# Order of halves in the first turn and at the router's first step, another schedule for the pieces of the late shared experts, and shared parts added by one transfer

## The reference, cut to what matters

```
x = x + cross_attention(layernorm(x), ctx)          # 16 query heads, 8 key/value heads of 128, 256 context rows
h = layernorm(x)
scores = sigmoid(h @ gate_w.T); sc = scores + gate_bias      # 32 experts in 4 groups
group_scores = top2 of each group, summed; keep the 2 best groups; topk_idx = best 4 experts
topk_w = scores[topk_idx] / sum * 2.0
experts: at most 128 rows each, (silu(h @ w1[e]) * (h @ w3[e])) @ w2[e], weighted by topk_w
shared:  (silu(h @ shared_gate) * (h @ shared_up)) @ shared_down
x = x + experts + shared
```

## Time and profile before

| | us |
|---|---|
| median of three runs | 1691.13 |
| profiled execution | 1686.83 |
| its span, first to last instruction | 1685.1 |
| PE busy | 1618.0 (96%) |
| DVE busy | 1223.4 (73%) |
| POOL busy | 887.6 (53%) |
| ACT busy | 787.4 (47%) |
| mean granted clock of TensorE | 0.991 of full speed |

### The profile page before, as it was taken

The page is one execution under the profiler, slowest core; times in us unless marked ns, Lnnn a source line. Parts: engine busy times, 40 slices in busy tenths (PEclk is TensorE's granted clock), DMA queues, the critical chain, the costliest instruction groups (busy, mean ns, idle before and its releaser), DMA issues. The chain is left out here.

```text
span 1685.1 us, 34839 instructions
## 1 busy us (share of the span) xinstructions
PE 1618.0 (96%) x12194; PEld 1153.3 (68%) x12194; DVE 1223.4 (73%) x3498; ACT 787.4 (47%) x1986; POOL 887.6 (53%) x1188
## 2 busy tenths in 40 slices
PE   6999999999999999999999999999999999999983
PEld 4767677777777777767676767776776766555541
DVE  6887676767676776767676777777777765787872
ACT  5764444435343444444443544445454433565551
POOL 2444544545463636464545463646455356677773
PEclk9999999999999999999999999999999999999997
DMA  7654433344344434343335544445454385799974
GB/s 233 184 143 79 89 80 80 82 76 96 64 96 76 96 61 92 70 102 67 80 74 97 93 95 92 102 95 108 90 112 83 88 319 155 207 281 281 275 194 59
DMA packets 394461, 204.12 MB, mean 121 GB/s; under 512 B 347808, under 2 KB 356000, under 8 KB 394288
## 3 DMA queue, kind: packets, MB, share of 16 engines
q1 hardware_dynamic: 380416, 180.27, 44.4%
q0 software_dynamic: 13312, 20.57, 6.6%
q10 hardware_dynamic: 560, 1.05, 0.2%
HBM read 87.15 MB, written 31.36 MB: 70 GB/s over the span
## 5 line engine op out<-in xcount | busy, mean ns | idle before, releaser
L961 ACT ACTIVATE arena<-arena,neg_max 128x256 f32<-128x256 f32 x512 | 253.7, 496 | 384.7 <-DVE neg_max L1260 331.5
L690 POOL TENSOR_SCALAR arena<-arena,prob_scale 128x256 f16<-128x256 f32 x384 | 184.5, 496 | 461.2 <-DVE prob_scale L1269 447.1
L1260 DVE CUSTOM_DVE_ANT_0 arena<-ps_score,mask_add 128x256 f32<-128x256 f32 x512 | 186.6, 421 | 141.7 <-PE ps_score L1606 141.7
L1604 PE MATMUL ps_query<-xn_both,arena 128*128 128x256 f16 x1024 | 279.2, 273 | 1.6 <-DMA xn_both<-xn_half 1.6
L1606 PE MATMUL ps_query<-xn_both,arena 128*128 128x256 f16 x1024 | 279.1, 273 | 0.0
L1605 PE MATMUL ps_query<-xn_both,arena 128*128 128x256 f16 x1024 | 279.1, 273 | 0.0
L1275 DVE SCALAR_TENSOR_TENSOR arena<-arena,prob_scale 128x256 f16<-128x256 f32 x384 | 233.0, 654 | 8.2 <-POOL arena L690 8.2
L1604 PE MATMUL ps_out<-arena,o_t 128*128 128x512 f16 x512 | 194.1, 379 | 0.7 <-DVE o_t L1280 0.7
L1605 PE MATMUL ps_out<-arena,o_t 128*128 128x512 f16 x512 | 194.0, 379 | 0.0
L1606 PE MATMUL ps_out<-arena,o_t 128*128 128x512 f16 x512 | 194.0, 379 | 0.0
L745 POOL DMA_INDIRECT slot_table<-entry,slot_at x128 | 133.2, 1041 | 48.2 <-issue 33.4
(11 more groups left out here) (319 smaller groups left out, 4110.7 us busy)
## 6 DMA issues: line engine op xcount, KB each, us to landing
arena<-w SPq DMA_DIRECT2D x96, 512.0 KB
x_in<-x SPq DMA_DIRECT2D x16, 512.0 KB, 4.0
xn_rows<-xn_half SPq DMA_DIRECT2D x15, 512.0 KB, 3.1
out_rows_dram<-x SPq DMA_DIRECT2D x30, 256.0 KB
ctx_in<-ctx_t SPq DMA_DIRECT2D x16, 256.0 KB, 3.1
weight_in<-wq SPq DMA_DIRECT2D x8, 512.0 KB, 5.8
weight_in<-wo SPq DMA_DIRECT2D x8, 512.0 KB, 4.6
arena<-arena SPq DMA_TRANSPOSE x256
```

The lines of the kernel that those rows point to most:

```text
L690: pool.tensor_scalar(p_rows[:, c, 0, :], probs[:, c, :], prob_scale[:, c:c + 1], 1.0, ALU.mult, ALU.mult).then_inc(norm_hi, 1)
L961: act.activation(probs[:, c, :], probs[:, c, :], ACT.Exp, bias=neg_max[:, c:c + 1], scale=-1.0, accum_out=prob_sum[:, c:c + 1]).then_inc(e ...
L1260: dve.tensor_tensor_reduce(out=probs[:, c, :], in0=ps_score[h][:, t * S:(t + 1) * S], in1=mask_add[b % 2][:, :], scale=-SCORE_SCALE, scala ...
L1604: pe.matmul(dst, a.hi, b.hi, start=start and n == 0, stop=False)
```

## The change

Six things change.

1. The first turn. x of sequence 0 is loaded as two transfers, so that its first rows can be measured alone. ctx_low(0) goes behind xn_rest. PE does value(0,0,0) before scores(0). value_low and ctx_low(1) of the first turn go from before prob_scales to behind it: the first behind prob_scales, the other two behind key_low(1). ACT does the second value_high behind scale_last.
2. The order of `jobs`: of wq and wo for the same head, wq is loaded and split first.
3. In every turn head_low(i-1) is done after two of the three low halves of the probabilities (late_head is gone).
4. At j = 3 choose_0 and choose_1 are done after query_low and key_low instead of around query_low.
5. The pieces: two up pieces instead of one before the two down pieces of the sequence before. NOT_BY_POOL and the orders of DVE, ACT and POOL around it follow. POOL does record(z-1, 1) after six splits and the first expert_high instead of first. The first gather is used after piece 20 instead of after piece 21. Pieces beside experts lie in steps with e % 8 != 7, so e = 0 to 21; the shared parts n = 5, 6 are added in step 22.
6. add_shared is one transfer of 256 rows instead of two of 128.

```diff
 for _n in range(len(LATE)):
-    PIECES.append(("u", _n, 0))
+    PIECES += [("u", _n, f) for f in range(2)]
     PIECES += [("d", _n - 1, t) for t in range(TB)] if _n else []
-    PIECES += [("u", _n, f) for f in range(1, FSB)]
+    PIECES += [("u", _n, f) for f in range(2, FSB)]
...
-NOT_BY_POOL = (10, 13, 14, 15, 16)
+NOT_BY_POOL = (10, 11, 14, 15, 16)
...
-    if _e % 4 != 3 and EARLY + len(BESIDE) < len(PIECES):
+    if _e % 8 != 7 and EARLY + len(BESIDE) < len(PIECES):
...
             def add_shared(n):
-                for t in range(TB):
-                    r = LATE[n] * T + t * P
-                    pool.wait_ge(staged, TB * n + t + 1)
-                    if t == 0:
-                        pool.wait_ge(out_rows, 16 * TB * (LATE[n] + 1))
-                        if n > 2:
-                            pool.wait_ge(added, adds_before["s", n])
-                    pool.dma_start(out[r:r + P, :], shared_y[n % 2][t], accum_op=ALU.add).then_inc(
-                        added if n else added_first, 16)
+                r = LATE[n] * T
+                pool.wait_ge(staged, TB * (n + 1))
+                pool.wait_ge(out_rows, 16 * TB * (LATE[n] + 1))
+                if n > 2:
+                    pool.wait_ge(added, adds_before["s", n])
+                pool.dma_start(out[r:r + T, :].rearrange("(t p) d -> p t d", p=P), shared_both[n % 2],
+                               accum_op=ALU.add).then_inc(added if n else added_first, 16)
...
 (pool_program, after the last turn)
             z = B - 1
-            record(z - 1, 1)
             for k in range(3):
                 late_split(k)
             inv_std(1, z, x1_stats, x1_rstd, x1_normed)
-            for k in (3, 4):
+            for k in (3, 4, 5):
                 late_split(k)
-            for e in range(2):
-                expert_high(e)
-            for k in range(7, 10):
+            expert_high(0)
+            record(z - 1, 1)
+            expert_high(1)
+            for k in (8, 9):
                 late_split(k)
...
 (dve_program, a turn)
-                if i == 0:
-                    value_low(ps_fill[1], 0, 0, 0)
-                    value_low(ps_fill[0], 0, 0, 1)
-                    ctx_low(1)
...
-                if i and not late_head:
-                    head_low(i - 1)
+                if i == 0:
+                    value_low(ps_fill[1], 0, 0, 0)
                 if live:
                     probs_low(i, range(0, CELLS // 2))
-                if i and late_head:
+                if i:
                     head_low(i - 1)
                 if live:
                     probs_low(i, range(CELLS // 2, CELLS - 1))
-                if j == 3 and routed:
-                    choose_0(z)
                 if i + 1 < TURNS:
                     query_low(i + 1)
-                if j == 3 and routed:
-                    choose_1()
...
                 if i + 1 < TURNS and not early_key:
                     key_low(i + 1)
+                if i == 0:
+                    value_low(ps_fill[0], 0, 0, 1)
+                    ctx_low(1)
+                if j == 3 and routed:
+                    choose_0(z)
+                    choose_1()
...
 (pe_program, after the last turn; act_program the same with copy_rows)
-            for k in range(11, EARLY):
+            for k in range(11, EARLY - 1):
                 piece(k)
-            for e in range(2):
-                expert_rows(e)
+            expert_rows(0)
+            piece(EARLY - 1)
+            expert_rows(1)
```

More of the change, by code:

```diff
@@ L830, in pool_program @@
                 gather(e)
-            for k in range(19, EARLY):
+            for k in (20, 21):
                 late_split(k)
@@ L1438, in dve_program @@
                 xn_rest(0, t)
+            ctx_low(0)
             for n in (0, 1):
@@ L1486, in dve_program @@
                     find_slots(z)
-                late_head = i < TURNS and first(b, j) is not None and first(b, j)[0] in ("value", "down")
                 if live:
@@ L1541, in dve_program @@
             piece(4)
-            for part in (0, 1, 2):
+            piece(5)
+            for part in (0, 1):
                 expert_low(0, part)
@@ L1826, in pe_program @@
                 b, j = divmod(i, KV)
+                if i == 0:
+                    filler(("value", 0, 0, 0), ps_fill[1])
                 if i < TURNS:
```

56 lines of the change are left out of this document (33 added, 23 removed).

## The result

The changed kernel takes 1702.86 us (median of four runs, 1700.55 to 1703.7) beside 1691.43 of the kernel before: ratio 1.0067, 95% interval 1.005 to 1.0085. It is 11 us slower, where 1684 was forecast. The profiled executions are 1700.55 (span 1698.8) against 1686.83 (1685.1), 13.7 apart.

A forecast was written before the change was run, and what follows sets the result against it. The prediction took TensorE, busy for 96% of the span, plus its idle stretches to bound the kernel. Its terms, 0 + 9.5 - 4.8 - 11.9 = -7.2 us, applied to the 1691.1 median gave 1684 us, range 1671 to 1695.

The forecast's parts named there:

- First turns: Start of attention: earlier second scores not kept, since project(0) waits for head_low; 0, from -3 to +3 us.
- Late head: Attention turns, mainly from b=10: head_low behind two probability halves holds project until 2.48 us after GpSimd's start; +18.8 us.
- Choose behind the key: Attention at j=3 of b=10 to 15: the 1.00 us wait of the next scores goes; -6.0 us.
- the attend waits: Inside attention: waits for the turned probabilities, 3.4 us, shrink as the turns before them get longer; -3.3 us.
- Router's last step: Between attention and experts: splits ahead of records bring the first expert from 1425.4 to 1420.6; -4.8 us.
- Experts: Expert steps to the end: fewer losses in the first 22 steps, faster accumulating transfers behind; -11.9 us, bounds 0 and -18.
- (1): Rival, groups after e=22: adds bind the bare steps, each us of spacing above 9.5 costs 5; 1696 us, chance 0.22.
- (3): Rival, router and start: gather chain doesn't move, start loses 2 us to a fallen clock; 1691 us, chance 0.11.
- (2): Rival, attention: late head is cheap, gaining up to 9.3 us, sum -20 or more; 1668 us, chance 0.10.
- (4): Rival, attention: VectorE's low and GpSimd's high halves hinder each other, 0.2 us a turn, +5; 1689 us, chance 0.07.

The follow-up runs named there:

- late_only: Kernel before with only head_low(i-1) put behind two low halves of the probabilities in every turn; ratio 1.0109 to the kernel before, +18.6 us.
- combo_old_start: combo with the first turn, the load of x and the order of weight jobs of the kernel before; ratio 0.9943 to the kernel before.
- choose_only: Kernel before with only choose_0 and choose_1 put behind query_low and key_low at j = 3; ratio 0.9959 to the kernel before, -7 us.
- changed_again: The changed kernel run again without an edit, beside the other follow-up runs; ratio 1.0080 to the kernel before.
- second pair: Traces of the unedited changed kernel and kernel before, both run again in the follow-ups; ratios 1.0080 and 1.0005 to the kernel before.
- old_steps: Changed kernel with pieces back in the steps of the kernel before (e % 4 != 3), shared parts n = 5, 6 in step 26; ratio 1.0043.
- combo_old_steps: combo with pieces in the steps of the kernel before (e % 4 != 3), shared parts in step 26; ratio 0.9915 to the kernel before.
- bare_20: Changed kernel with step 20 also left without a piece; ratio 1.0038 to the kernel before.
- piece21_first: Changed kernel with piece 21 put back before the first rows on TensorE and ScalarE; ratio 1.0062 to the kernel before.
- combo: Changed kernel with head_low back in its early place, step 20 without a piece and piece 21 before the first rows; ratio 0.9914 to the kernel before.

## Why the prediction was wrong

- **First turns, 0.** Within its bounds (+0.9 us at scores(8) by the first pair of traces, 0.0 by the second), and by the reason given: the lead of scores(1), 2.1 us for the 3.1 forecast, isn't kept, since project(0) and its followers wait for head_low. So 0 is a gain of 2 to 3 us by the new start less as much for the late head, as late_only and combo_old_start show.
- **Late head, +18.8.** Right in place: 2.47 to 2.49 us in each bound turn. In size it is right where it is part of the changed kernel (next point). That late_only's runs give +18.6 is in part luck: the 18.8 is a sum before the 3.3 us of waits that go with it, so 15.5 was to be compared with 18.6 (interval 15.6 to 20.9), and the traces show 13.6. What the Trainium skill's page "SBUF — State Buffer", section "Who interferes with whom", would make of it, by the prediction's estimate about 2.7, isn't what the turns show; with both engines at it project came 2.47 to 2.49 behind.
- **Choose behind the key, -6.0, and the attend waits, -3.3.** Right together: choose_only -7; scores(80) to (127) +8.1 in the changed kernel and +8.3 in changed_again, for 17.9 - 9.3 = 8.6. Attention as a whole came to +11.3 for +9.5, and to +9.5 in the second pair.
- **Router's last step, -4.8: failed,** +2.5 in the first pair, -1.9 in the second. What failed is the sentence that the first gather's rows land at about 1416.8, 3.9 us behind their issue, with TensorE there 1.6 us before. From issue to rows it was 7.2 (changed) and 6.9 (changed_again). In the kernel before it was 6.1 already (1416.88 to 1423.0), and TensorE came just as the rows landed, so no wait showed it. TensorE then stood 4.96 or 3.66 us ahead of the rows, with piece 21, 2.6 us of ready work, queued right behind them, and its clock fell. From the first copy to the first tanh it was 4.4 us before, 7.5 after. By terms, from scores(127): the gather was forecast at 65.5, its rows at 69.4 and the first tanh at 75.9. The first trace has it issued 1.9 later, landing 3.3 slower and the tanh another 2.1 later, 7.3 in all; the second -1.6, +3.0 and +1.4, or 2.7. So the landing was mis-sized by 3 us in both; the late issue, behind the split of piece 17, was in the first alone. With the piece ahead of the rows the step gains 4.0 (76.5 for 80.5).
- **Experts, -11.9: failed,** 0 in the first pair, +1.6 in the second. Two terms. The first 22 steps were put at 166.0 and took 172.9: I had counted bare steps only as room for additions and not asked what stands between the last hidden row and its down piece; with no bare step there GpSimd's split is late, 5.98 us and the clock behind it. The rest from step 22 was put at 81.8 and took 86.6 (1698.8 less 1612.2): the shared additions were issued at 11.7 for 9, and landed in 16.4 for 13; the six pairs behind them and the end came as forecast. 6.9 + 4.8 is 11.7 of the 11.9. That the stage came out at 0 is itself a sum: the dense steps lost some 4 us against old_steps, and the rest of the change seems to have given as much back.
- **The rivals.** (1), the additions bind the bare steps, did not come by its own measure: the five distances behind the first pair were 9.4 us on average, (1687.33 - 1640.36)/5, where it priced what lies above 9.5. What was long was the landing of the shared ones ahead of them. And yet combo_old_steps shows that the schedule is worth nothing with the additions in the way: what the wait in step 20 costs less, the end takes back in part. (3) is what the first pair looks like at the router by its time, but not as a mechanism: the last record was issued 2.3 us earlier behind scores(127), 4.1 in the second pair. (2) and (4) are refuted by the 2.48.
- **Slips in the working,** none of which changes the account: 3.1 and 1.6 less 0.5 is 4.2, not 4.5; by its own price (1) breaks even at 10.9 us, not 11.1; and (2) with its 9.3 makes -16.5, 1675 us and not 1668.

Forecast and trace are 20.9 us apart (-7.2 and +13.7): 1.8 in attention, 7.3 at the router's last step, 11.8 in the experts. Both failed steps were sums in which several waits had to go without a new one in their place.

What stays open: in which stage a faster execution of the kernel before gains the 5 us that its traces lack; which part of the change gives the experts some 3 us; and why VectorE's halves, and with them the split of piece 17, came later in the first trace of the changed kernel than in the second.

## What to carry to other kernels

Where an edit changes the order of two instructions that gate a loop, look for a turn in which the new order is in force already: its distance from release to user (2.48 us here) held to 0.01 in every later turn that it bound. Where two edits touch the same turn, price them together: choose behind the key gave 7.0 us at j = 3 with the early head and 3.4 with the late one. A step that waits for a transfer's landing is priced from issue to use, and from the trace only if the user stood waiting there; where it didn't, the landing may be anything up to its arrival, and ready work belongs ahead of it. Before a schedule is made denser, ask of each empty slot who used it to catch up; and where a chain of dependent transfers runs beside the work, finishing the work earlier may only buy waiting. And before a trace is compared with another, see where its own execution lies among the runs: here one stood 5 us above the median that it was to stand for.

## What the runs showed of the hardware

Behind a wait of TensorE of 4.96 us its granted clock was 0.75 over 8 us, and behind one of 5.98 us 0.50 from 1596.5 to 1601.8, that is, 1.2 GHz instead of 2.4; in bare_20 taking away the wait of 5.98 us gave 8.1. Behind one of 3.66 us it was 0.82 over 8 us. The length of the wait alone doesn't decide it: behind 2.16 us (piece21_first) the clock stayed at 1.00, and behind 1.85 us at the same place in combo it was 0.50 for 2.7 us (1410.19 to 1412.90). An indirect gather of 128 rows (the first one, in all seventeen traces) took 6.0 to 7.3 us from issue to use, with a DMA share of 0.97 around it in the changed kernel. Pairs of shared additions (1 MB) landed in 9.1 to 16.7 us, the long ones while expert weights were being loaded (DMA share 1.04 at 297 GB/s from 1624 to 1640), and one or two transfers for each made no difference. Two executions of the same program differed by 4.6 us in the router's step.
